# Row sums of the cross attention taken by the accumulator of ScalarE's exps instead of by a VectorE reduction, with a new written-out order of steps

## What is computed

```
x = x + L0_attn(norm(x))            # "self0": causal, 16 heads of 8
x = x + L0_xattn(norm(x), ctx)      # "cross0": 8 heads of 64, output bias
x = x + L0_ffn(norm(x))             # "ffn": ternary weights, rounded activations
x = x + L1_attn(norm(x))            # "self1": causal, 16 heads of 8, scores clipped to +-10
x = x + L1_xattn(norm(x), ctx)      # "cross1": 16 heads of 64
x = x + L1_ffn(norm(x))             # "moe": 8 experts of 128x128, gated by a softmax with threshold 0.1
```

## Time and profile before

| | us |
|---|---|
| median of 3 runs | 531.2 |
| lowest, highest | 529.69, 532.6 |
| profiled execution, its time | 529.94 |
| its span in the trace | 528.2 |

### The profile page before, as it was taken

How to read it: one execution, slowest core, us unless ns; L and a number is a source line. 1 busy time by engine, 2 the same in 40 slices (tenths; PEclk the granted TensorE clock), 3 DMA queues, 4 the chain that set the end, 5 groups by cost and what they waited for, 6 DMA issues and landing times.

```text
span 528.2 us, 15974 instructions
## 1 busy us (share of the span) xinstructions
PE 497.7 (94%) x5490; PEld 419.3 (79%) x5490; DVE 409.2 (77%) x923; ACT 441.3 (84%) x1177; POOL 395.2 (75%) x570
## 2 busy tenths in 40 slices
PE   4998989999999999999999999999999999988884
PEld 2876777777988888788888888888988898777762
DVE  3857778887788987979788897889878887786552
ACT  5987789999888888989899888988978898887831
POOL 5785778787678987888868785898778687776454
PEclk9999999999999999999999999999999999999995
DMA  6800000000000000000000000000000000000000
GB/s 195 327 4 1 1 2 3 2 2 2 2 2 6 3 2 7 8 2 3 7 1 2 4 6 7 1 6 4 6 2 2 7 7 2 6 7 2 6 6 11
DMA packets 6463, 8.96 MB, mean 17 GB/s; under 512 B 1008, under 2 KB 4848, under 8 KB 6384
## 3 DMA queue, kind: packets, MB, share of 16 engines
q1 hardware_dynamic: 6384, 7.94, 4.6%
HBM read 6.50 MB, written 1.05 MB: 14 GB/s over the span
## 4 chain that ended last, share of the span: by engine, by line
PE 70%; POOL 8%; issue 7%; POOLq 6%; ACT 4%; DVE 3%; DVEq 1%; ACTq 0%
PE S L1132 11%; PE S L1119 7%; PE X L1076 7%; PE X L1159 7%; PE X L1187 7%; PE S L1106 5%; POOL diff_cross L672 4%; PE X L1292 2%; PE X L1145 2%; PE X L1198 2%; PE X L1170 2%; PE X L1172 2%; PE X L1171 2%; ACT diff_cross L747 2%; PE X L1178 2%
## 5 line engine op out<-in xcount | busy, mean ns | idle before, releaser
L667 POOL TENSOR_TENSOR w_low_self<-w_self 128x1024 f16<-128x1024 f32 x64 | 120.7, 1896 | 15.8 <-ACT w_self L736 10.9
L672 POOL TENSOR_TENSOR diff_cross<-diff_cross,e_rec_cross 128x1024 f32<-128x1024 f32 x48 | 91.0, 1898 | 24.8 <-DVE e_rec_cross L898 24.5
L747 ACT ACTIVATE diff_cross<-S,row_max_cross 128x128 f32<-128x128 f32 x384 | 103.8, 404 | 4.3 <-DVE row_max_cross L889 3.6
L889 DVE TENSOR_REDUCE row_max_cross<-S 128x8 f32<-128x1024 f32 x48 | 57.9, 1215 | 18.2 <-PE S L1119 17.7
L896 DVE TENSOR_REDUCE e_sum_cross<-diff_cross 128x8 f32<-128x1024 f32 x48 | 58.2, 1213 | 3.9 <-ACT diff_cross L747 3.2
L756 ACT ACTIVATE w_cross<-S 128x1024 f32<-128x1024 f32 x48 | 49.7, 1039 | 8.4 <-PE S L1132 8.0
L1119 PE MATMUL S<-kT_cross,qT_cross 64*128 64x128 f32 x768 | 54.6, 283 | 0.2 <-ACT qT_cross L712 0.2
L1119 PEld LDWEIGHTS S<-kT_cross,qT_cross 64*128 64x128 f32 x768 | 46.4, 187 | 7.3 <-issue 4.5
L1159 PE MATMUL X<-w_cross,v_cross 128*64 128x128 f32 x768 | 51.7, 278 | 0.1
L1132 PE MATMUL S<-ident,diff_cross 128*128 128x128 f32 x384 | 50.3, 274 | 0.9 <-POOL diff_cross L672 0.8
L1159 PEld LDWEIGHTS X<-w_cross,v_cross 128*64 128x64 f32 x768 | 41.1, 136 | 11.0 <-issue 5.7
(11 more groups left out here) (191 smaller groups left out, 1396.7 us busy)
## 6 DMA issues: line engine op xcount, KB each, us to landing
out_dram<-x_all SPq DMA_DIRECT2D x16, 64.0 KB, 1.5
x_all<-in_x SPq DMA_DIRECT2D x1, 768.0 KB, 7.3
cT_all<-in_ctx SPq DMA_DIRECT2D x1, 768.0 KB, 9.0
e_k<-in_e_k SPq DMA_DIRECT2D x1, 512.0 KB, 4.9
e_v<-in_e_v SPq DMA_DIRECT2D x1, 512.0 KB, 6.0
e_q<-in_e_q SPq DMA_DIRECT2D x1, 512.0 KB, 9.0
e_o<-in_e_o SPq DMA_DIRECT2D x1, 512.0 KB, 11.3
m_w<-in_m_w SPq DMA_DIRECT2D x1, 512.0 KB, 9.0
```

Of the source, the lines that this page charges most:

```text
L667: pool.tensor_tensor(L.w_low[u][:], L.w[u][:], halves(L.w[u][:]), ALU.subtract)\
L672: pool.tensor_tensor(L.diff[u][:].rearrange("p (h k) -> p h k", h=UNIT), L.e[u][:].rearrange("p (h k) -> p h k", h=UNIT), L.e_rec[:, u, :] ...
L747: last = act.activation(L.e[u][:, P * p:P * (p + 1)], S_[:, P * p:P * (p + 1)], ACT.Exp, bias=L.row_max[:, u, p:p + 1])
L889: dve.tensor_reduce(L.row_max[:, u, :], group(i, turn)[:].rearrange("p (h k) -> p h k", h=UNIT), AX_X, ALU.max, negate=True).then_inc(L.ma ...
```

## The change

In `cross_exps` each of the eight activations gets `accum_out`, so that it also leaves the sum of its 128 exponentials in one column of `e_sum`. In `reciprocal_sums` the reduction and its drain go, and the reciprocal alone is left; what it waits for is unchanged. The costs in `all_steps` become 2540 for `ex` (2060 before) and 200 for `rc` (1401 before). The order strings of PE, DVE, ACT and POOL are new: of 721, 405, 679 and 277 places in these lists, 132, 111, 102 and 76 hold the same step of the same sequence as before. SP's list is the same.

```
-            add(f"{L}.ex.{c}", "ACT", 2060, [f"{L}.mx.{c}"], [f"{L}.t.{c}"])
-            add(f"{L}.rc.{c}", "DVE", 1401, [f"{L}.ex.{c}"])
+            add(f"{L}.ex.{c}", "ACT", 2540, [f"{L}.mx.{c}"], [f"{L}.t.{c}"])
+            add(f"{L}.rc.{c}", "DVE", 200, [f"{L}.ex.{c}"])
...
 ORDER = dict(
     PE=(
-        "aHaLaJaHa4aOa4a6a6a4a4bqaUa6aQaJbWbWbYbWbWaXaObYaLbYb0b0aHaUb2bYaQaZa6b2aJa1a4b0aXaOaZbab2aLaHb2bcaJ"
+        "aHaJaLa4a4aOa6aHa4a4a6aUa6bqaJaQbYbYbWbWbWaXaOaLb2aHbWaZbYaUb0b0aQa1aJbYb2a6a6aXaOaZbaaLa4aHbcaJa1aU"
...
                 for p in range(UNIT):
                     last = act.activation(L.e[u][:, P * p:P * (p + 1)], S_[:, P * p:P * (p + 1)], ACT.Exp,
-                                          bias=L.row_max[:, u, p:p + 1])
+                                          bias=L.row_max[:, u, p:p + 1], accum_out=L.e_sum[:, u, p:p + 1])
                 last.then_inc(taken(i, turn)[0], 1)
...
                 dve.wait_ge(*taken(i, f"{L.name}.s1.{u}"))
                 if i:
                     dve.wait_ge(L.diff_ready[u], i)
-                dve.tensor_reduce(L.e_sum[:, u, :], L.e[u][:].rearrange("p (h k) -> p h k", h=UNIT), AX_X, ALU.add)
-                dve.drain()
                 dve.reciprocal(L.e_rec[:, u, :], L.e_sum[:, u, :]).then_inc(L.rec_ready[u], 1)
```

More of the change, by code:

```diff
@@ new lines @@
+        "b0aQbeb2b2aXaOaZa4aLa6baaUbcaHa1bjaQaJbebla4a6bnaXaOaZaLbaaHa4bcaUa1b0bwbjbyaQbeblbCbEbGbnaXaJbJaZba"
+        "aLaHbcbja1beblbwa6bybna6bQaOa4bCbSa4babEbUaUbcbjbwaQaJbyblbGb6bJcab8bebCccaXaLclbQaZa6bnbjbSa1bEbUch"
+        "blbGaHbJcjb6b0b8cqcaccbwbacsclbYbybQbnb2bYbSaObCbWbWbcbUbGaUbEcucqaQb6bwaJbecscha4byaXcab8aZbJaLcycj"
+        "ccclcBa1cua4b2cCbCa6bjbQbEcGaHaOblcybaa6b0bnbSaQbGbUbcaUcKcBcqaJbecCb6csb8chaXcabJaLaZcjccclbwa1b2cu"
+        "bQbYbybjaHbWbWaOblbabCbYcGbEbGaUbSbncKbUcyaQbccqcBb0chbeb6aJcCb8aXcabJcscjccaZaLbwcla4byb2cua1bjbQaH"
@@ new lines @@
+        "aObSbCcGblbUbEbaaUbnbGcycKcqcBaQb6bcb8bJcGaJcacCaXchbeaLbwaZcccscjbQa1byclb0cucKbjbWbWaHaOblbSbYcyb2"
+        "bUaUbCbabncBbccqaJaQbGbEbeb6cCcaaXchb8csbJb2cjccaZbwaLcla4bya1cua4bjbYbQaOblaHbaa6bSb0cGbCaQbnbGcyaJ"
+        "aUcKbUchbccqcBa4bEbwbecjb6cCbyaXcab8aLbJaZcGbCcsccaHcla1cub0bQbjbWbWbEaObSb2bYbYblcybaaUbUbccBaQcKcq"
+        "bGaJbeb6bncCcaaXchaLb8cGaZbJaHa1csclcjccbwb2cubjbybQa6a6aObSbablcybCbcbUaQcBaJbncqbEbGaUcKbeb6cCcab8"
+        "chb0aXbJcjcscccGbwaZclb2bya1cubQaLbjbYbWaOblbSbabWa6bCaUbGbUaHbccyaQcqcBbnaJchbEbeaXcKcCcjcsaOaZaLb6"
@@ L199 @@
+        "b0b0b8cGaQcabwa1aUclb2bycccKcuaXbjbYaZbabJa1cybccBcqbCblbecsbabEcCbnbcchbQb0bJcjbSb2bjbUbGbecub6bwbl"
+        "byb8cacGcccKcybCclcBbQbnbWbjb0bWcCbSbEbGchcGbUcqblcjbJb6bwcsb8bycaccclcKbnbCcubQbYbYbScyb0bEcBbUchbG"
+        "cCbwcqb6cjbyb8bJcabCcGcccsclbEb2cubQbGbJcybSbUchcBcKcqcCb6cjcscabQclb8bSbUccb6cucqb8cachcccGcycKclcj"
+        "cscBcCchcucqcGcjcscycKcBcucCcGcycBcKcCcGcK"
     ),
     DVE=(
-        "aEaEaraEataEavaTbpaPbraEaYaTaPa2aYaTaPbfa2aEbhaTaYaPa2bfboaEaYbhaTbuaPbxaEbza2bfbobhaYbNbubKbxa2aEbf"
@@ L202 @@
[L202 to L206, removed]
@@ L207 @@
-        "cdbzcvcoaYcfbNcAa2cDbKcFbobfcLcIbRbhbubNbKbVbxbfbzcvcLbhcdcmbocfcAbRcocDbucFbVcIbobxbNbzbKcdbucvcmcf"
-        "cLbxbRcocAcDbVcFbzcIbKbNcdcmcLcvcfbRcobNbKbVcAcDcFcIbRcmcdbVcocfcvcdcLcmcfcAcDcocFcIcvcAcDcLcFcvcIcD"
+        "aEaEarataEavaTbpaPbraEaYaTaPa2aEaYaTaPbfaEa2aYbhaTaEaPa2bfboaYbhaTbuaPbxbza2bfaEboaYbhbNaEbKbua2bfbx"
+        "bzbobhbRaTbuaPbVbxbzbNbKbfcdbhaYcmcfbRboa2cobVbKbNbucdbxaEcmbzbRbococfaTbubVaPaEbfbxcvbzaYbhbNbKcdcm"
+        "a2cAcDcvcFcIcocfbRaPcAaTbVcLcDbocFbfcIbuaYbhbKbNcda2bxcmcvbRbzcfcoaTaPbobVcLaEcAcDbubfcFcIbhaYbNbKcd"
@@ new lines @@
+        "bxcmbzcfa2cvbRcoaTbVaPcLcAcDbocFbNbubKcIaYbfbxaEcdbhbRcmbza2cvcocLcfaTcAbVaPcDboaEcFbfcIaYbubNbhbKcd"
+        "bxcma2cfbzcvbRaPcoaTboaEcAcLbVbucDbxbfcFbzcIaYbhbNbKcdcmcva2cfbRcoaTaPbVcAcDcLcFaEbfbocIbhaYbubNbKcm"
+        "cda2bxcocvbzbRaPcfcAbVaTbocDcFbfcIcLbubhaYbKbNcdbxcmbza2cvbRcfcoaTaPbVcDcAbocFbfcLcIaYbubhaPaTa2bxcm"
+        "bzcdcLcvcoaYbKa2bNcAcDbfcfcFbocIbhbRbubNbKbVbfbxcvbzcdcAbhcLcmbRcDcfbococFcIbVbubKbxbNbzcdcmcLbocfcv"
+        "bRcocAbucDbVcFbxcIbzbKbNcdcmcvcfcobRbNbKbVcAcLcDcFcIbRcmbVcdcocfcvcdcAcLcmcfcocDcFcvcIcDcAcFcvcLcIcD"
@@ L211 @@
     ACT=(
[L212 to L225, removed]
+        "aGaqasaIaKauaGa5a5aIaMa7a5a5awaVa7a7ayaRbZaKbXaGaAbZbXbXaMaIaGbXb3a0aVb1bZb1aRaKbZaCb3a7a9a7aMa0bbaI"
@@ new lines @@
+        "bdaGa5aVb1aKaRbgb3b3a9aMa0bba5aVbda7aIbkaRaKbmbgaGa9a7a5aMa0btbbaIa5bdbvaVaGbkaRb1bBbmbDbgbFa9bHaKbb"
+        "bta0bObdaMbkaIbvbLbmbgbBaGa7a7a9btbDbTbba5bFaVbvbda5bkaRb5bmb7bHaKbBcbbOb9bLbDbgceaMa0cnbTbkbFcia9bH"
+        "bma7aIb5aGbtb7bLb1ckb9crbvbOcbbbcebZcnctbTbBbZb3btbXbDbXbdbHbvaVbFb5craRb7aKctbgcia5cxb9a0bBcbaMczbO"
+        "bLckcecEcnbDb3a5a7bkbFa9cxcHaIbmczbbaGb1a7bTaRbHbdaVcEcraKb5b7btbgcibvcbb9ctaMa0bLbOckceb3cnbka9aIbX"
+        "bZbBcxbXbbbDbmcHbZbFbHbTaVaGczaRbtbdcrcEbvb5cib7b1bgb9aKcbctbObLckaMa0cecnbkb3a5aIbBcHbTbDa9bmcxbFbb"
@@ new lines @@
+        "aVbHczb5crcEb7aRbdb9aGbtbOcbaKbvcHcibLaMa0bgckctcecnbkaIbXbXb1cxa9bmbTbBczbZb3aGbbaVbDbdcEcrb5aRbHbF"
+        "b7bgcbcibtaKb9bvctb3bOckbLa0aMcecnbka5a5a9bZbBaIbbbmbTa7b1cHbDcxaRbHczaKaVbtciaGbvbdcra5b5cEbFckb7bg"
+        "cbaMbBb9a0cHbDbOctbLaIcecnbkb1bXbXcxbFbTb3bZa9aGbZbmbbczaVbdcEaRb5crbHaKb7bgcbbtcia0bvaMb9cHaIbOctbL"
+        "ckcncebka9a7b3a7bBcxbTbbbmbDczbdaRaKb5crbHcEaVbFb7btbgcib9cbbvb1ckbLbOcHa0ctcecnbkaMbZaGb3bBa9bXbTbm"
+        "cxbXbDbba7bHaVbdczaRaIcEcraKcibFbgckbtctb5bva0b7aMb1b9b1aRcHcbaVa9cncebkbZbba0cxb3czbBbdbLcrbDcEbma9"
@@ L226 @@
+        "bObbbgbFcibtctbdb1bTckbObvbkbLbHb5b3b7bgb9cxcHcbbBbmczbDcecncEbXb1bkbTbXbFcibtcrbHcHbvb5ckbmb7bLb9ct"
+        "cbbObBcecnbZcxbDbTbtczbZb1cEbvcibHb5bFb7crb9ckbBcbbLbDbOctcebFcncxcHbHb3bTczbOcibLb5crcEb7cbckctbTb9"
+        "cnb5ceb7b9crcicxcbcHczcecnctckcEcicrcxckcHczctcEcxczcEcHcH"
     ),
     POOL=(
-        "apaFaFaFaFaNaxaWaSazaBaNaWaSa8aDaNaFaWaSa8aNa3a3biaWaFaSbsa3a8biaFaNaWbAaFaSa8bsbibIbPa3bMa8bAbsaFbI"
-        "biaNaWb4bAaSa3bMbPbsbicgaNa8a3b4bIcpbPbMbAbscgcpaFaWb4aSbAcwa8bibMbIbPcgaNa3cwcJcpaSbsb4aWaFbIcJbiaN"
@@ L230 @@
[L230 to L233, removed]
+        "apaFaFaNaFaxaWaSazaFaNaBaWaSa8aFaNaWa3aSaDaFa8biaNa8aWaSa3bsaNbiaFaWbAa8aSaFbsbia3bIbPa8bMbAaNbsbiaW"
@@ new lines @@
+        "b4bAbIaFaSbPa3bMbicga8bsb4cpbIa3aNbMbPbAa3bsaFcpcgb4aWaScwbAbiaNbMbIa8bPcwcpa3cgcJb4aSbsbIaWaFcJbibM"
+        "bPa8cwa3bAcpcgaNbIbsb4aWaSaFcJbibMbPbAaNcwa8cpcgb4bIaWa3bsaSbPbMcJbiaNa8cwbAcpaFcgb4aWbsaSa3cJbIbPaF"
+        "bibMa8bAaNcwcgcpbsb4aSbIaWa3bAaFbibPbMcwa8cJcga3cpb4aNaWaSbIbsbiaFcJbPbMaNa8cwbAcpb4aScgbsaWcJbia3bI"
+        "bMbPbAa8cwcgcpaWaSaNb4bscJaNbibIa8aSaWa3bAcwcpa3a8bMcgbPbsbicJb4bIbPcwbAbMbia3cgcpbsb4bIcJbAbMbPbscw"
+        "cgcpb4bIbAcJbMbPcwcgbIcpb4bPbMb4cpcgcwcJcgcpcwcJcwcJcJ"
```

## The result

The change makes the kernel slower, by more than the range allowed: 544.2 us at the median (544.12 to 545.5) beside 530.7 us. The ratio is 1.026, with a 95% interval of 1.024 to 1.028. That is 13.5 us more. The profiled execution took 544.12 us with a span of 542.4 us, 14.2 us above the span before.

The account below looks back on a forecast made before the run. The prediction took PE as full in the middle and bounding the kernel. Terms of -0.4 (layout changes), -1.3, -0.3 and +2.0 summed to 0.0 us against 529.94; with the 531.2 median it took 530.5 us, range 522 to 540.

Parts of the forecast that it names:

- I add 95 ns to each, to 348 ns: Cross exps on ScalarE: each accumulator read adds 95 ns to 253 ns, 36.5 us over 384 reads.
- is worth nothing: VectorE's relief of 62.1 us, in the middle beside a full PE, gains no time.
- 2 us, with 0 and 10.9 as ends: Middle, 106 to 449 us: loss from ScalarE's longer exps, taken as 2 us, between 0 and 10.9.
- -1.3: First stretch: a reduction on the chain at 63.92 us goes, saving 1.3 us, bounds 0 and 2.9.
- -0.3: Last stretch: one single unit gains 0.53 us, one pair loses 0.2; ends +1 and -3.7 us.
- The ceiling of 94.4%: Middle: ScalarE's possible highest busy share with PE fed, from the densest half window; would need 353.9 us, 10.9 more.
- priced at nothing: New order of steps: collisions unreadable from the old trace, so 0 us, left to the range; layout changes separately -0.4 us.
- a price of 60 ns a read: Planner's cost in the diff, 480 ns a unit, used as lower bound for the reads: 23 us in all.
- B: Rival: ScalarE takes over the middle, copies reach PE late; about 539.5 us, chance 0.32 at full or half price.
- A: Rival: VectorE's relief pays at both ends, nothing lost in the middle; about 523.5 us, chance 0.22.
- C: Rival: PE is not full, so its middle shrinks with the faster softmax; at best 519.0 us, chance 0.05.
- D: Rival: the accumulator is free, ScalarE neither gains nor loses; same time as A, chance 0.03.

Follow-up runs that it names:

- sums, old order: Kernel before with only the softmax edit (exps accumulate, VectorE's reduction gone), its order and costs kept: 561.3 us, ratio 1.055.
- small copies behind the release: Kernel before plus eight small unused ScalarE copies after each cross unit's exps, behind the release of the S group (the PSUM buffers they hold): 561.2 us, ratio 1.058.
- no sums: Kernel before, old order, without accumulation or VectorE's reduction; the reciprocal is taken of the row maxima: 528.6 us, ratio 0.996.
- new order alone: Kernel before with the changed kernel's order of steps, old softmax and costs kept: 553.4 us, ratio 1.042.
- order for 2790: Changed kernel with lists written anew for 2790 ns instead of 2540 for a unit's eight exps with reads: 535.6 us, ratio 1.009.
- order for before: Kernel before with its own softmax and costs, its lists searched anew by the same means: 527.0 us, ratio 0.992.
- all reads: Kernel before, old order, every cross exp accumulates while VectorE's reduction is kept and used: 564.1 us, ratio 1.063.

## Why the prediction was wrong

*The pieces were sized right.* "I add 95 ns to each, to 348 ns": measured 90 and 343. VectorE's relief "is worth nothing" in the middle; the run without sums gives 2.0 us in all. ScalarE's busy total rose by 29.2 us, to 470.5 instead of 478, since parts of the records overlap. By the Trainium skill (ScalarE: Activation LUTs, "What ACT_TABLE_LOAD costs") back-to-back activations overlap by about 93 ns, from which the estimate of 103 ns for a read of 196 came; the trace has 90 from start to start, so the rule was near.

*The step that failed* is the price of ScalarE's longer exps in the sum. They were charged only in the middle, where PE was seen to be full, at "2 us, with 0 and 10.9 as ends". At the ends they were set against the unit's own saving: "-1.3" for the first stretch and "-0.3" for the last. In the changed kernel the three stretches came out at +5.8, +3.3 and +5.1 us. The new order is in these numbers too. The runs in the old order show the term without it. Here are the three stretches of each profiled execution, cut at the starts of sequences 6 and 14, as differences from the kernel before:

| version | starts of 6 and 14, us | first | middle | last |
|---|---|---|---|---|
| sums, old order | 136.81, 384.89 | +6.7 | +11.6 | +13.2 |
| small copies behind the release | 134.37, 382.35 | +4.2 | +11.5 | +14.3 |
| no sums | 129.90, 365.53 | -0.2 | -0.8 | +0.4 |
| new order alone | 136.80, 380.76 | +6.7 | +7.5 | +8.7 |
| changed kernel | 135.96, 375.71 | +5.8 | +3.3 | +5.1 |
| order for 2790 | 134.93, 372.89 | +4.8 | +1.5 | -0.5 |
| order for before | 130.46, 366.80 | +0.3 | -0.1 | -3.9 |

So the longer exps cost more than the whole stated span of 0 to 10.9 us even in the middle, and 20 us more at the two ends. VectorE's relief alone, which was to carry the -1.3 and the -0.3, came to +0.1 us at the two ends together. At the ends the exps do not hold up only their own unit. Behind them in ScalarE's queue stand the copies for all the other sequences, and PE gets its input later. PE's waits in the last stretch show it, in the kernel before and then with the copies behind the release, which come after the exps that the unit's own sums wait for (L1106 and L1109 are the same line):

```profile
PE S L1106 <- ACT by_head_self L712: 1.6, 1, 1.6
```

```profile
PE S L1109 <- ACT by_head_self L712: 3.1, 1, 3.1
PE X L1190 <- ACT attnT_cross L712: 1.5, 1, 1.5
PE X L1201 <- ACT kT_cross L712: 1.3, 1, 1.3
```

The columns are the total, the number and the longest of the waits, in us. The second and third are not among the seven longest before, which are of 0.9 us and more. These are three waits of many; no run adds them up to the 14.3 us.

One reading was also slightly off: the window from 449 to 529 us runs 0.8 us past the end of the span, so PE's idle time there is 16.7 us and not 17.5. Nothing hangs on it.

*The ceiling of 94.4% fell as well.* In the old order with the sums, ScalarE is busy in the middle for less than that ceiling, and PE is idle all the same (from 106 to 449 us):

```profile
106.00:449.00 343.00, 327.11 (x3725) 278.71 (x3724) 233.64 (x576) 314.08 (x1066) 255.19 (x359) 1.00 0.01 4
```

That is 91.6% for ScalarE and 15.9 us of idle PE. With the order laid out for the real durations it is 95% with 1.0 us of idle PE between the marks. So no share of busy time is the limit; the order decides how much of a share can be used.

*The new order was priced at nothing.* Alone it is worth +22.8 us, and with the sums -17.1. It could not be read from the old trace, but the range of 18 us should have been wider for it. The two do not add up as separate terms: an order that suits one set of durations is a bad one for the other. The kernel's own table had a price of 60 ns a read against the 95 that the rows gave; I used it as a bound for the cost, and did not ask what lists laid out for 60 do with 95. Written anew for the real price they give back 8.6 of the 13.5 us, of which the further search has a part that is not separated (it gave 3.8 us to the kernel before).

*The rivals.* B had the right sign and mechanism, at 539.5 us, with the loss put in the middle alone. It took its size from the ceiling that fell. In the old order the middle did lose 11.6 us, near B's 10.9, but at a load of ScalarE below that ceiling, so the nearness is luck. A, C and D did not happen. For C: the changed kernel's period did not shrink (29.97 us for a sequence in the middle, 29.56 before). The Trainium skill's rule on weight-load time (Perfetto Trace Analysis, "Identifying the Most-Contended Engine") would have given PE room in the middle; freeing VectorE of 54 us found 2.0 us in the whole kernel, and the order searched for the kernel before left the middle at 236.3 us (236.5 before), so the traces do not bear it out here.

*A part that stays open: TensorE's clock.* In the kernel before, the granted clock is 1.00 up to 516 us and falls only in the last 12 us. In the changed kernel it is at 0.50 (1.2 of 2.4 GHz) in two more places. The first two rows are of the kernel before, the others of the changed one:

```profile
0.00:516.00 516.00, 492.65 (x5476) 416.01 (x5476) 405.62 (x909) 440.15 (x1172) 390.57 (x563) 1.00 0.05 17
516.00:528.20 12.20, 5.02 (x14) 3.34 (x14) 3.61 (x14) 1.14 (x6) 4.59 (x8) 0.53 0.04 12
```

```profile
48.00:50.00 2.00, 0.89 (x32) 0.89 (x32) 0.51 (x3) 2.00 (x13) 2.00 (x2) 1.00 0.00 0
50.00:57.00 7.00, 6.59 (x44) 4.22 (x41) 4.90 (x9) 2.39 (x8) 5.87 (x10) 0.51 0.00 0
...
482.00:484.00 2.00, 0.90 (x8) 0.34 (x8) 0.94 (x3) 2.00 (x10) 1.97 (x2) 0.87 0.00 0
482.00:491.00 9.00, 7.48 (x34) 5.66 (x35) 4.97 (x13) 6.39 (x18) 6.89 (x8) 0.62 0.02 7
```

Just before the first fall and around the second, PE was busy for only 0.89 and 0.90 of 2 us, while ScalarE was busy for the whole of them. An estimate from these rows: 6.59 x 0.49 and 7.48 x 0.38 make 6.1 us of longer matmuls, about the 6.0 us by which PE's busy total grew. So the loss has two parts, 8.2 us in which PE waits and some 6 us in which it works more slowly. That the clock fell because PE waited fits the order of events, but it is argued and no run shows it. With only the price changed, the clock is 1.00 from 50 to 56 us and falls from 110 to 115 us instead, and again from 482 to 490; the order for 2790 has falls near 24 and 462 us. None of the experiments isolates what the clock costs, and the copies and reads in the old order carry it too (PE's busy total is 14.2 us longer with all reads).
